# A gated cross-attention and low-rank block: the first context converted once per chunk into f16 words, its column sums taken in 32-column strips, x1 of three tiles evicted ahead of its correction

## What is computed

```
q1 = clip(round(layernorm(x) / s1 + z1), 0, 255);  q2 = clip(round(ctx / s2 + z2), 0, 255)
x  = x + tanh(g0) * ((q1 - z1) * s1) @ ((q2 - z2) * s2)
x  = x + tanh(g1) * layernorm(x) @ (U * S @ V.T).T
```

## Time and profile before

| | |
|---|---|
| three executions | 601.25, 601.6, 601.85 us, median 601.6 |
| profiled execution, span from first to last instruction | 600.8 us |
| TensorE busy, VectorE, ScalarE, GpSimd | 97%, 64%, 35%, 32% |
| granted clock of TensorE in every slice | 0.9 or more, mean 1.000 |
| moved by DMA | 102.7 MB |

### The profile page before, as it was taken

One profiled execution on the slowest core, in us unless ns is written; L12 is line 12 of the kernel. 1 busy time (PEld: TensorE's weight loads), 2 busy tenths in 40 slices (PEclk: granted clock), 3 DMA queues, 4 the chain that ended last, 5 costly groups with the idle time before them and its releaser, 6 DMA issues.

```text
span 600.8 us, 7536 instructions
## 1 busy us (share of the span) xinstructions
PE 583.0 (97%) x2800; PEld 266.3 (44%) x2800; DVE 384.5 (64%) x703; ACT 210.5 (35%) x256; POOL 193.5 (32%) x149
## 2 busy tenths in 40 slices
PE   1999999999999999999999999999999999999998
PEld 0444444444444444445444444444444444444444
DVE  6968999995288962855266975647375665735212
ACT  4799877822041432476422220303011030301000
POOL 2998850002223419735505800210404030030000
PEclk9999999999999999999999999999999999999999
DMA  8999995539828896979934432360917355171512
GB/s 275 387 387 386 308 262 127 109 122 196 242 54 230 192 217 189 274 264 327 235 123 140 102 73 54 75 189 12 211 42 157 106 97 166 32 161 35 123 53 105
DMA packets 145940, 102.74 MB, mean 171 GB/s; under 512 B 108784, under 2 KB 109040, under 8 KB 145904
## 3 DMA queue, kind: packets, MB, share of 16 engines
q1 hardware_dynamic: 136912, 84.96, 53.6%
q10 hardware_dynamic: 8992, 17.30, 8.8%
HBM read 58.99 MB, written 16.78 MB: 126 GB/s over the span
## 4 chain that ended last, share of the span: by engine, by line
PE 74%; DVE 12%; DMA 7%; issue 3%; ACT 1%; SPq 1%; POOL 1%; ACTq 0%; DVEq 0%
PE bank L556 27%; PE bank L587 14%; PE bank L654 8%; PE bank L653 8%; PE bank L658 8%; PE bank L592 7%; DMA v_hl<-in_ctx_dram 4%; DVE u_hl L1249 2%; DVE ring L1134 2%; DVE xn L1171 1%; DVE xs L1174 1%; DVE v_hl L1243 1%; DMA qT<-qn 1%; PE bank L519 1%; DMA ring<-in_x_dram 1%
## 5 line engine op out<-in xcount | busy, mean ns | idle before, releaser
L556 PE MATMUL bank<-q,qT 128*128 128x512 bf16 x896 | 202.1, 381 | 0.6 <-DVE ring L1134 0.3
L556 PEld LDWEIGHTS bank<-q,qT 128*128 128x128 bf16 x896 | 87.7, 98 | 107.9 <-issue 1.8
L260 POOL TENSOR_SCALAR ring<-ring,bvec 128x2048 f32<-128x2048 f32 x16 | 33.3, 2084 | 270.2 <-DVE bvec L1116 270.2
L587 PE MATMUL bank<-v_hl,xT 128*128 128x512 f16 x512 | 115.8, 379 | 0.0
L265 POOL TENSOR_TENSOR ring<-ring,corr 128x512 f32<-128x512 f32 x64 | 88.7, 1417 | 24.6 <-ACT corr L851 23.6
L1134 DVE SCALAR_TENSOR_TENSOR ring<-bank,const,ring 128x512 f32<-128x512 f32 x64 | 47.6, 743 | 57.9 <-PE bank L556 57.8
L1207 DVE SCALAR_TENSOR_TENSOR ring<-bank,cy,ring 128x512 f32<-128x512 f32 x63 | 46.6, 747 | 56.7 <-PE bank L658 56.6
L654 PE MATMUL bank<-u_hl,hbuf 128*128 128x512 f16 x208 | 78.9, 380 | 0.0
L653 PE MATMUL bank<-u_hl,hbuf 128*128 128x512 f16 x208 | 78.9, 379 | 0.0
L254 POOL TENSOR_SCALAR q<-u8r,const 128x1024 bf16<-128x1024 uint8 x52 | 64.2, 1243 | 39.2 <-ACT u8r L757 35.6
L587 PEld LDWEIGHTS bank<-v_hl,xT 128*128 128x128 f16 x512 | 49.9, 98 | 59.9 <-DMA xT<-xs 0.5
(11 more groups left out here) (136 smaller groups left out, 524.9 us busy)
## 6 DMA issues: line engine op xcount, KB each, us to landing
out_dram<-ring SPq DMA_DIRECT2D x63, 256.0 KB, 3.6
ring<-in_x_dram SPq DMA_DIRECT2D x62, 256.0 KB, 4.1
v_hl<-in_ctx_dram SPq DMA_DIRECT2D x26, 512.0 KB, 11.5
stage<-in_ctx_dram ACTq DMA_DIRECT2D x17, 512.0 KB, 5.5
u_hl<-in_L_ffn_V_dram SPq DMA_DIRECT2D x8, 512.0 KB, 11.4
corr<-in_ctx_dram ACTq DMA_DIRECT2D x8, 512.0 KB, 6.1
stage<-in_ctx_dram SPq DMA_DIRECT2D x6, 512.0 KB, 11.4
q<-in_ctx_dram ACTq DMA_DIRECT2D x4, 512.0 KB, 10.1
```

Source lines behind the costliest of these rows:

```text
L556: mm = nc.tensor.matmul(unit_bank(t, n)[:, :], qT_of(t)[:, k, :], q2[:, n, k, :], start=(k == 0), stop=(k == KT - 1))
L587: nc.tensor.matmul(h_bank(u)[:, :], xT[:, g, half, k % 8, :], v_hl[:, k, 0, :], start=(g == 0 and a == 0 and half == 0), stop=False)
```

## The change

All in the first context, and around it:

- q2, qn, qT, the identity and the ones are f16 in place of bf16. q2 holds 1024 + q: every two-byte word is filled ahead with a constant whose bits are those of 1024, and the conversion writes its clipped byte into the low byte of the word (`q2_low`). One step per chunk, no u8r. The fills: q2[0], q2[1] and, later, q2[3] by GpSimd (L242 of the new file, 4096 elements of four bytes), q2[2] by VectorE as its first instruction.
- Chunks 6, 7, 8 and the even ones from 10 on go to ScalarE, the rest to GpSimd; VectorE has none.
- The column sums of the first context are taken in strips too, two chunks at a time, and totalled: `colsum_total(0, n-1)` stands in TensorE's order behind chunk 2 of quarter n, that of quarter 3 between s1(1,3) and s1(2,3).
- For tiles 0 to 2, VectorE adds S1 first (`x1_evict`, it waits for `pre_row`), GpSimd's `pre` waits for it and for the correction, and the statistics come apart, later (`x1_stats`).
- `norm_sums(0)` goes behind s1(3,1) in TensorE's order. On VectorE `norm_sum_up(0)` and `norm(0)` go behind x_lo of tile 0 and the unit (3,0). In SP's order the transpose of tile 3 goes ahead of V's loads and that of x of tile 0 ahead of U's quarter 0.
- The identity isn't rebuilt as f16 on GpSimd.

The diff, cut to its core:

```diff
+            def fill(n):
+                nc.gpsimd.memset(flat2(q2[:, n, :, :]).bitcast(f32), OFFSET_PAIR).then_inc(q2_filled, 1)
+            def op1(c):
+                pool.wait_ge(SPOT[c][1], LANDED[c])
...
+                nc.gpsimd.tensor_scalar(q2_low(c), flat2(SPOT[c][0]), C_R2, P_Z2, ALU.mult, ALU.add).then_inc(q2_pool, 1)
...
             def pre(t, n):
-                pool.wait_ge(x1_row, t + 1)
+                if t < G:
+                    pool.wait_ge(x1_ready, unit(t, n) + 1)
+                else:
+                    pool.wait_ge(x1_row, t + 1)
...
+            fill(0)
+            fill(1)
             for c in range(CQ):
-                if not on_dve(c):
-                    op2(c)
+                if c not in ON_ACT:
+                    op1(c)
             for n in range(NQ - 1):
-                for i, c in enumerate(range(CQ * (n + 1), CQ * (n + 2), 2)):
-                    op2(c)
+                for i, c in enumerate(range(CQ * (n + 1) + 1, CQ * (n + 2), 2)):
+                    op1(c)
                     if n == 0 and i < G:
                         pre_row(i)
+                if n == 0:
+                    fill(3)
                 for t in range(G):
                     pre(t, n)
...
+            q_transpose(G)
             for i in range(CQ):
                 load_v(VORD[i])
-            q_transpose(G)
             u_load(2)
             u_load(3)
+            x_transpose(0)
             u_load(0)
-            x_transpose(0)
...
             for n in range(1, NQ):
                 for i in range(CQ):
-                    colsum(0, n, CK * i, CK * i + CK)
+                    if i % 2 == 1:
+                        colsum(0, n, CK * i - CK, CK * i + CK)
                     for t in range(G if n < NQ - 1 else 1):
                         s1_part(t, n, CK * i, CK * i + CK)
+                    if i == 2:
+                        colsum_total(0, n - 1)
             s1_part(1, NQ - 1)
-            s1_part(2, NQ - 1, 0, 8)
+            colsum_total(0, NQ - 1)
+            s1_part(2, NQ - 1)
+            s1_part(G, 0)
+            s1_part(G, 1)
             norm_sums(0)
-            s1_part(2, NQ - 1, 8)
-            s1(G)
+            s1_part(G, 2)
+            s1_part(G, 3)
             mm3(0)
...
-            for j in VORD[0:5]:
-                v_square(j)
+            v_square(VORD[0])
+            v_square(VORD[1])
+            column_parts(0, 3)
+            v_square(VORD[2])
+            v_square(VORD[3])
             column_correction(0, 3)
-            for j in VORD[5:8]:
+            for j in VORD[4:8]:
                 v_square(j)
             root2(0)
+            x_hi(0)
             weight_root(0)
-            x_hi(0)
             for i in range(VP):
                 v_high(i)
             root2(1)
...
+            nc.vector.memset(flat2(q2[:, 2, :, :]).bitcast(f32), OFFSET_PAIR).then_inc(q2_filled_dve, 1)
...
+            x1_evict(0, NQ - 1)
+            column_low(0, NQ - 1)
+            for t in range(G):
+                x1_stats(t, NQ - 2)
+            x1_evict(1, NQ - 1)
+            x1_evict(2, NQ - 1)
+            x1_stats(0, NQ - 1)
             variance2(0)
-            norm_sum_up(0)
             scale2(0)
-            norm(0)
-            x1_unit(1, NQ - 1)
-            x1_unit(2, NQ - 1)
             x_lo_half(0, 0)
             x_lo_half(0, 1)
+            x1_stats(1, NQ - 1)
+            x1_stats(2, NQ - 1)
             x1_unit(3, 0)
+            norm_sum_up(0)
+            norm(0)
             v_low(0)
             variance2(1)
             v_low(1)
             scale2(1)
             for i in range(2, 4):
                 v_low(i)
             x_lo_half(1, 0)
             for i in range(4, VP):
                 v_low(i)
             x_lo_half(1, 1)
```

275 lines of the change are left out of this document (131 added, 144 removed).

## The result

The changed kernel takes 613.23 us in the median of four executions (612.49 to 614.03) against 601.73 for the kernel before beside it: a ratio of 1.0189, 95% interval [1.0174, 1.0203]. It is 11.5 us slower. The forecast was 610.1 with a range of 604 to 614. The profiled execution has a span of 610.7 us, where 609.3 was forecast. Its own device time is 612.49, 1.8 us more than its span, and the two differ by 1.75 to 1.87 in every execution whose both numbers are listed; so the profile of the kernel before, with its span of 600.8, is that of an execution of about 602.6 us (an estimate from these differences), and not of its median. One of the seventeen executions of the kernel before beside e12 took 1265.7 us and is left out of the ratio.

A forecast was written before the change was run, and what follows sets the result against it. TensorE, busy 97% of the span, was taken as the bound, but the VectorE/ScalarE chain from V's last square sets the end: 111.4 - 102.8 = +8.6, taken as +8.5, span 609.3, forecast 610.1 us, range 604 to 614.

The forecast's parts named there:

- The direction and its main reason: Slower, chance 0.88: from V's last square one program-order chain through the late norm sets the first context's end, +8.6 us.
- The chain from the last square S: From V's last square on ScalarE, through x_lo(0), norm, v_high and scale2(1), to x_lo_half(1,1)'s end: S+33.0, at 111.4 us.
- TensorE's own work, -8.3: Column sums: 64 matmuls out (13.8 us), 64 strips (3.8) and 8 totals (1.7) in: net -8.3 us if nothing waits.
- First gate: At quarter 0's total, TensorE stands 4 us for VectorE's column parts, behind GpSimd's row correction of tile 2.
- Second gate: GpSimd's fill (3.5 us) and corrections delay chunks in quarters 2 and 3; s1(2,3) ends near 75.0, gain left 2.6.
- Third gate: Transpose ahead of V's loads delays V by 4 us, so ScalarE's last V square ends at S = 78.4, setting the end.
- From the chain's end to the time: After x_lo_half(1,1) the lag stays: +8.6 less a tenth gives +8.5, span 609.3 us, median 610.1.
- The forecast's 0.8: The 0.8 us by which the executions' median lay above the profiled span, added to span 609.3 to forecast 610.1.
- The signs that were named: TensorE idle 4 us at first total, 8 to 11 in 90-110; V squares awaiting DMA until 76-78; x_lo_half(1,1) near 111.
- B: Rival: conversion into every second byte takes twice its 1.2 us, s1(2,3) ends at 83, time 616; chance 0.09.
- A: Rival: norm chain off the path, TensorE's 8.3 us come off, time 593.3, needing S below 70; chance 0.08.
- C: Rival, a wash: V lands so much earlier that S comes near 70, time 600.4 to 602.8; chance 0.03.

The follow-up runs named there:

- e12: e11 with U-norm sums back ahead, column_parts(0,3) before V's squares, V's loads before the transpose, V-norm sums behind s1(3,0), two statistics moved: 601.76 us against 601.92.
- e5: The kernel before with only the V norm's sum and the norm of expert 0 moved late, as in the changed kernel: 609.13 us against 602.24.
- e7: The changed kernel with the sixteen column-strip matmuls of quarters 1 to 3 in one block each instead of four blocks of four: 611.94 us against 602.24.
- e9: The changed kernel with e7's blocks and the norm of expert 0 back ahead of x_lo(0), its sums inside s1(3,0): 605.00 us against 601.90.
- e6: The changed kernel with GpSimd waiting between its first two fills for VectorE's quantisation centre: 614.20 us against 602.24.
- e1: The changed kernel with V's eight loads again ahead of the transpose of tile 3 in SP's queue: 613.35 us against 601.97.
- e11: e9 with (3,0)'s eviction between x_lo(0)'s halves, U-norm sums inside mm3(1), e6's gap and GpSimd's rows and corrections reordered: 604.14 us against 601.90.
- e3: The changed kernel with root2(1) on ScalarE moved from behind the eighth v_high to behind the third: 614.88 us against 601.97.

## Why the prediction was right, and where it was not

**The direction and its main reason: right, and shown.** The norm of expert 0, moved behind x_lo(0) and the first quarter of tile 3, sets the end. Two kernels show it from both sides: its place alone put into the kernel before costs 6.9 us (e5), put back in the changed kernel with e7's blocks it returns 6.6 to 6.9 (e9). The chain from the last square S: +33.0 was forecast, 33.6 measured. Its steps, forecast against measured: scale2 done +1.4, +1.2; x_lo(0) +7.6, +8.7; (3,0) and statistics +10.3, +11.2; norm +12.0, +12.7; v_high +20.4, +21.2; scale2(1) +21.7, +22.4. The term that was short is x_lo(0): the subtraction took 1.42 and 1.64 beside GpSimd, not 0.8 to 1.2.

**TensorE's own work, -8.3: mis-sized.** The term for the strips, 3.8 for 64, was taken from strips in long runs. By four among S1's matmuls they cost 0.42 a block, 6.7 for sixteen blocks. The net was about -5.4, and e7 measured 1.3 to 1.8 us at the end for three of the four quarters.

**First gate, "it stands 4 us": it didn't show.** The gate is there, but something hid it. GpSimd's row of tile 2 ended at 39.7 (forecast 41.1), VectorE's eviction waited 0.66 for it, and the column parts were through at 41.1; TensorE reached its total only at 42.51, 1.4 us after the gate had opened. The whole start was late by the 3.67 us for which the fills held VectorE; the prediction allowed up to 4 us there and said that they would vanish in this gate, which is what happened. e6, with the start mended, shows the gate itself: 2.60 us, then a slower clock. The late start and the gate do not add up: the later of the two counts.

**Second gate: GpSimd as forecast, and TensorE later than it.** The fill took 3.5, as chosen, and chunk 31 was converted at 65.05, forecast 65.2. But TensorE, behind by its late start and its strips, didn't wait for it: tile 0 ended at 69.4 where 67.2 was forecast, and s1(2,3) at 76.7 for 75.0.

**Third gate, "V's landing sets S = 78.4": the step that failed.** S was 79.0, so the number held, and its cause did not; that it held was luck, since two costs that were left out (the strips' price and the late start) stood in for one that did not show. ScalarE's timeline shows the correction of quarter 3 waiting 1.53 us for TensorE's total, and four squares without a wait behind it; e1, with V ahead of the transpose, changes nothing. The prediction had the right setter at hand, "ScalarE waits for TensorE's column sums and total and S = 76.8", as its lower bound; with the strips' true price and the late start that bound moved up to 79. The landing became a wait only once TensorE was earlier (4.14 us in e11), and turning the order round made TensorE wait for the transpose instead (2.67 us in e12): the two share one queue, and either costs the other. What the transpose costs V's loads is in the two traces: with it ahead V landed 2.7 to 2.8 us later than in e1, where 4 was taken, and its last load at 75.0 where 76.8 was forecast.

The Trainium skill, DMA: Bandwidth & Descriptors, Latency and other measured facts, gives a DMA transpose 261 GB/s; by that the transpose would cost 2.0 us and not 4 (an estimate). The 2.7 to 2.8 lie between the two, beside other traffic; by e1 neither figure could change the time here. No run shows the rate of a transpose alone; the issue of this one held SP 6.64 us in the changed kernel and 10.03 in e12.

**From the chain's end to the time: 3.1 us short.** 1.2 to 1.4 at the end of the context (x_lo_half(1,1) at 112.6 for 111.4, mm3(1) at 112.03 for 110.6, the span 610.7 for 609.3), and 1.7 since the median lies 2.5 above the profiled span here, where it lay 0.8 above it before. The second part comes from which executions were profiled. An execution's time is 1.8 above its span throughout; so the one profiled before took about 602.6, some 0.9 above the median, while the one profiled of the changed kernel is the fastest of its four, 0.7 below the median. The other three have a granted clock of 0.989 to 0.992 where it has 0.997; what slowed TensorE in them no trace shows. The forecast's 0.8 was thus the difference between one execution and a median, and no constant.

**The signs that were named.** x_lo_half(1,1) ended at 112.6, near 111, and behind 125 us nothing differs: both came. TensorE idle 4 us at the first total and V's squares waiting for DMA until 76 to 78 us did not come. TensorE idle by 8 to 11 us in 90 to 110 came in part: it was busy 15.1 of the 20 us, thus idle 4.9, with another 2.20 just before, and part of the rest was paid in matmuls at a granted clock of 0.91 in the mean.

**The rivals.** B fell at once: the conversion into every second byte takes 1.20 on GpSimd and 1.23 on ScalarE, as the packed one. A needed S below 70 and C near it; even e12, with everything moved out of the way, has S = 74.1.

**What the change is worth, then.** In place of -8.3 us on TensorE it has -5.4, and with the blocks of e7 about -7.2 (an estimate: 1.7 for quarter 0's strips, 3.2 for three blocks, 1.7 for the totals, against 13.8). Yet the time after e12, which has the blocks, is that of before. The gain went into four places, each seen in a run, though their shares were not all measured apart: the changing over to strips, VectorE held by the fills, the pauses of TensorE with the clock behind them, and the ring of waits between V, the transpose, the norm and tile 3. In the trace of e12, where the blocks and the start are mended, TensorE's waits between 60 and 104 us add up to 5.8 us, and the matmuls behind the longest of them took 1.7 more.

## What to carry to other kernels

When an operation is moved in a hand-written order, ask for each engine that waits for it what stands behind its wait; here a chain of a few small operations, one microsecond and a half long, put off 8.4 us of ScalarE's work by 12 us. A visible wait is not a price until the engine behind it has been followed (e3 removed 4.49 us of it and lost time), and a transfer's late landing costs only if nothing else is later (e1, then e11). Take the price of an instruction from a row in which it stands among the same neighbours.
